# One kernel, three edits: VectorE adds the second bias itself, three gate products in a row, two weights turned a turn later

## The reference, cut to what matters

```python
x = x + _L0_conv_ref(_gn(x), w_qkv, w_dw, w_proj, temperature)
x = x + _L1_conv_ref(_gn(x), gate_w, gate_b, w1, b1, w2, b2)

def _L1_conv_ref(x, gate_w, gate_b, w1, b1, w2, b2):
    scores = _softmax(x_flat @ gate_w + gate_b, -1)
    top_v, top_i = jax.lax.top_k(scores, 2)
    top_w = jax.nn.softmax(top_v, -1)
    present = (top_i[:, :, None] == jnp.arange(4)[None, None, :]).any(0)
    coef = jnp.einsum('ke,kbhw->ebhw', present, top_w)
    hdn = relu(jnp.einsum('bchw,edc->ebdhw', x, w1) + b1)
    y = jnp.einsum('ebdhw,eod->ebohw', hdn, w2) + b2[:, None, :, None, None]
    return jnp.einsum('ebohw,ebhw->bohw', y, coef)
```

## Time and profile before

| | |
|---|---|
| median of 3 runs | 169.03 us (168.38 to 169.12) |
| the profiled execution | 168.52 us, of which the span of the profile is 166.7 |
| busy in the span | PE 149.2 us (89%), DVE 140.5 (84%), ACT 110.8 (66%), POOL 64.6 (39%) |
| TensorE's granted clock | full in all 40 slices |
| HBM traffic | 23 GB/s over the span |

### The profile page before, as it was taken

How to read it: one execution, slowest core, us unless ns; L and a number is a source line. 1 busy time by engine, 2 the same in 40 slices (tenths; PEclk the granted TensorE clock), 3 DMA queues, 4 the chain that set the end, 5 groups by cost and what they waited for, 6 DMA issues and landing times.

```text
span 166.7 us, 3638 instructions
## 1 busy us (share of the span) xinstructions
PE 149.2 (89%) x1291; PEld 118.4 (71%) x1291; DVE 140.5 (84%) x385; ACT 110.8 (66%) x250; POOL 64.6 (39%) x77
## 2 busy tenths in 40 slices
PE   0499899999989999997999999979998979789973
PEld 0499799999989999996999998846653422223321
DVE  2887997769999899899999889766757979999993
ACT  3485298659496493793895638763949699867830
POOL 7040224505237067175167227205125014854530
PEclk9999999999999999999999999999999999999999
DMA  5682123410504105014013000000000000112113
GB/s 139 173 233 63 22 65 96 137 29 4 153 10 128 32 4 150 11 45 118 0 52 116 0 4 0 0 6 0 0 0 0 0 0 4 47 47 88 56 49 94
DMA packets 8698, 9.06 MB, mean 54 GB/s; under 512 B 3624, under 2 KB 7496, under 8 KB 8680
## 3 DMA queue, kind: packets, MB, share of 16 engines
q1 hardware_dynamic: 8536, 8.59, 18.7%
q10 hardware_dynamic: 144, 0.24, 0.5%
HBM read 2.28 MB, written 1.57 MB: 23 GB/s over the span
## 4 chain that ended last, share of the span: by engine, by line
PE 48%; DVE 22%; ACT 13%; issue 5%; POOL 4%; DMA 3%; SPq 1%; DVEq 0%; ACTq 0%
DVE v_acc L1316 6%; PE qk_ps L858 5%; PE qk_ps L860 5%; DVE h_mixed L1597 4%; ACT h_mixed L612 4%; PE mix_ps L976 3%; ACT hidden L584 3%; DMA x_sb<-in_x 2%; PE mix_ps L1142 2%; PE out_ps L953 2%; DVE stats L1270 2%; POOL x_sb L791 2%; PE qk_ps L847 2%; PE qk_ps L849 2%; PE qk_ps L848 2%
## 5 line engine op out<-in xcount | busy, mean ns | idle before, releaser
L1316 DVE SCALAR_TENSOR_TENSOR v_acc<-v_ps,v_taps,v_acc 96x544 f32<-96x544 f32 x60 | 46.6, 777 | 4.8 <-ACT v_acc L480 3.7
L858 PE MATMUL qk_ps<-w_a,x_a 128*128 128x192 f16 x243 | 46.6, 245 | 0.4 <-DMA x_c<-x_lo 0.4
L860 PE MATMUL qk_ps<-w_b,x_b 128*128 128x192 f16 x243 | 46.5, 245 | 0.0
L858 PEld LDWEIGHTS qk_ps<-w_a,x_a 128*128 128x128 f16 x243 | 24.5, 101 | 0.8 <-issue 0.7
L860 PEld LDWEIGHTS qk_ps<-w_b,x_b 128*128 128x128 f16 x243 | 23.6, 97 | 0.3
L1597 DVE TENSOR_TENSOR h_mixed<-h_mixed,hidden 128x512 f32<-128x512 f32 x24 | 21.4, 941 | 1.2 <-ACT h_mixed L612 1.2
L791 POOL TENSOR_TENSOR x_sb<-x_sb,xn 96x512 f32<-96x512 f32 x8 | 14.3, 1788 | 19.6 <-ACT xn L590 19.6
L863 PE MATMUL qk_ps<-w_c,x_c 96*128 96x192 f16 x81 | 20.1, 248 | 0.0
L753 POOL TENSOR_TENSOR sq_sum<-qk_sq 128x384 f32<-128x384 f32 x7 | 7.0, 999 | 29.6 <-ACT qk_sq L497 24.9
L556 ACT ACTIVATE sc_exp<-sc_qk,neg_max 96x12 f32<-96x12 f32 x16 | 4.7, 296 | 16.9 <-DVE neg_max L1361 16.9
L762 POOL TENSOR_TENSOR rstd<-var_eps,minus_half 96x2 f32<-96x2 f32 (+2 forms) x9 | 8.5, 944 | 19.1 <-DVE var_eps L1296 19.1
(11 more groups left out here) (228 smaller groups left out, 384.6 us busy)
## 6 DMA issues: line engine op xcount, KB each, us to landing
x_b<-x_a SPq DMA_DIRECT2D x7, 324.0 KB, 3.1
x_sb<-in_x SPq DMA_DIRECT2D x8, 192.0 KB, 3.9
out<-xs SPq DMA_DIRECT2D x7, 192.0 KB, 2.1
x_a<-x_lo SPq DMA_DIRECT2D x7, 108.0 KB, 2.4
x_b<-x_lo SPq DMA_DIRECT2D x7, 108.0 KB, 2.3
x_c<-x_lo SPq DMA_DIRECT2D x21, 36.0 KB, 1.9
w_sb<-in_L_conv_w SPq DMA_DIRECT2D x2, 144.0 KB
cst<-in_consts ACTq DMA_DIRECT2D x1, 236.0 KB, 3.6
```

What stands on the lines that cost most here:

```text
L858: eng.matmul(to, window(x_a[p][:, dx, b], half, dy), w_a[:, t, :], start=(t == 0), stop=False, skip_group_check=True)
L860: mm = eng.matmul(to, window(x_b[p][:, dx, b], half, dy), w_b[:, t, :], start=False, stop=False, skip_group_check=True)
L1316: eng.scalar_tensor_tensor(out=v_acc[i % 3][:, :, :], in0=v_window(dy, dx), scalar=v_taps[:, t:t + 1], in1=v_acc[i % 3][:, :, :], op0=ALU. ...
```

## The change

It has three parts. In the tail `b2_part` is gone from ACT, and the addition from POOL. DVE's new `add_bias(i)` reads w0's bank, multiplies by the first column of `bias_col` and adds `x_sb` in one instruction; `add(i)` also adds the second column. PE now waits for `x1_biased`, which DVE sets, before it overwrites w0's bank. In stage 2 `gate(5)`, `gate(6)` and `gate(7)` stand next to each other on PE, with `first(8)` and `first(9)` behind them, and ACT does the three `high_xn2` before `gate_exps(1)` and `relu(8)`. In stage 1 `prep_w1`, the turning of w1 and w2 and all that belongs to it stand one turn later.

```diff
@@ scalar, stage 1
-                if i == 5:
+                if i == 6:
                     copy_w1()
-                if i == 6:
+                if i == 7:
                     copy_w2()
@@ scalar, stage 2
-            relu(8)
+            high_xn2(5)
+            high_xn2(6)
+            high_xn2(7)
             gate_exps(1)
-            high_xn2(5)
-            relu(9)
-            high_xn2(6)
-            relu(10)
-            high_xn2(7)
-            for h in (11, 12, 13, 14):
+            for h in range(8, 15):
                 relu(h)
@@ scalar, tail
-            eng.wait_ge(bias_ready, 1)
-            bias_tile(0)
             top_exps(1)
             coefs(1)
-            bias_tile(1)
             for i in range(2, PAIRS):
                 if i == 3:
                     take_u(1)
                 coefs(i)
-                bias_tile(i)
@@ gpsimd
-            for i in range(PAIRS):
-                eng.wait_ge(b2_ready, i + 1)
-                eng.tensor_tensor(x_sb[:, i, :], x_sb[:, i, :], b2_part[i % 2][:, :], ALU.add).then_inc(x1_biased, 1)
@@ tensor, tail: weight(i)
-                    eng.wait_ge(b2_ready, i - 1)
+                    eng.wait_ge(x1_biased, i - 1)
@@ vector, stage 1
-                if i == 4:
+                if i == 5:
                     prep_w1()
-                if i == 5:
+                if i == 6:
                     low_w1()
@@ vector, tail
+            def add_bias(i):
+
+                eng.wait_ge(w0_done, i + 1)
+                eng.wait_ge(bias_ready, 1)
+                if i == 0:
+                    eng.wait_ge(x1_done, PAIRS)
+                eng.scalar_tensor_tensor(out=x_sb[:, i, :], in0=w0_ps[i % 2][0:C, :], scalar=bias_col[:, 0:1],
+                                         in1=x_sb[:, i, :], op0=ALU.mult, op1=ALU.add).then_inc(x1_biased, 1)
...
-                eng.tensor_tensor(out_sb[i % 2][:, :], x_sb[:, i, :], y_ps[i % 2][0:C, :], ALU.add).then_inc(y_taken, 1)
+                eng.scalar_tensor_tensor(out=out_sb[i % 2][:, :], in0=y_ps[i % 2][0:C, :], scalar=bias_col[:, 1:2],
+                                         in1=x_sb[:, i, :], op0=ALU.add, op1=ALU.add).then_inc(y_taken, 1)
```

More of the change, by code:

```diff
@@ L181, in build @@
         bias_col = sb("bias_col", [C, 2])
-        b2_part = xn2[0:2]
         h_mixed = [sb(f"h_mixed{p}", [128, MT, T]) for p in range(2)]
@@ L315, in build @@
         coef_set = sem("coef_set")
-        b2_ready = sem("b2_ready")
         x1_biased = sem("x1_biased")
@@ L585, in relu @@
                    .then_inc(hid_by_act, 1)
[L587 to L591, removed]
             def gate_exps(c):
@@ L816, in prepare_w1 @@
                 eng.wait_ge(w1_step, 5)
-                eng.wait_ge(mix_ready, 4)
+                eng.wait_ge(mix_ready, 5)
                 for m in range(MT):
@@ L822, in prepare_w2 @@
             def prepare_w2():
-                eng.wait_ge(mix_ready, 5)
+                eng.wait_ge(mix_ready, 6)
                 for m in range(MT):
@@ L936, in mix_heads @@
                     eng.wait_ge(proj_set, 1)
-                if a == 4:
+                if a == 5:
                     eng.wait_ge(w1_lo_set, 1)
-                if a == 5:
+                if a == 6:
                     eng.wait_ge(w2_set, 1)
@@ L1076, in _ @@
             gate(5, 0, 8, 24)
-            first(8)
             gate(6, 0, 8, 24)
-            first(9)
             gate(7, 0, 8, 24)
-            for h in range(10, 12):
+            for h in range(8, 12):
                 first(h)
@@ L1603, in add @@
                 wait(eng, stored[i % 2], 16 * (i // 2))
-                eng.tensor_tensor(out_sb[i % 2][:, :], x_sb[:, i, :], y_ps[i % 2][0:C, :], ALU.add).then_inc(y_taken, 1)
+                eng.scalar_tensor_tensor(out=out_sb[i % 2][:, :], in0=y_ps[i % 2][0:C, :], scalar=bias_col[:, 1:2],
+                                         in1=x_sb[:, i, :], op0=ALU.add, op1=ALU.add).then_inc(y_taken, 1)
             mix(0)
+            add_bias(0)
             mix(1)
+            add_bias(1)
             gate_weights(1)
@@ L1612, in _ @@
             add(1)
+            add_bias(2)
             for i in range(3, PAIRS):
@@ L1615, in _ @@
                 add(i - 1)
+                add_bias(i)
             for b in range(2):
@@ L1621, in _ @@
                 eng.wait_ge(stored[1], 16 * (PAIRS // 2 - 1))
-                eng.tensor_tensor(out_sb[1][:, t], x_sb[:, PAIRS - 1, t], y_last[b][0:C, t], ALU.add).then_inc(y_taken, 1)
+                eng.scalar_tensor_tensor(out=out_sb[1][:, t], in0=y_last[b][0:C, t], scalar=bias_col[:, 1:2],
+                                         in1=x_sb[:, PAIRS - 1, t], op0=ALU.add, op1=ALU.add).then_inc(y_taken, 1)
 def constants():
```

## The result

The changed kernel has a median of 164.61 us (164.06 to 164.92, four runs); the kernel before, on the same chip, 169.0 (168.38 to 169.12). The ratio is 0.9744, with a 95% interval from 0.9704 to 0.9784: faster. The profiled execution took 164.91 us with a span of 163.1. The forecast was 163.4 with a range from 162.2 to 165.8. The kernel before takes 168.3 to 169.2 us in 31 of its 58 executions beside the experiments, with a mean granted clock of 1.00, and 169.4 to 171.6 in the other 27, with 0.99 or less. Where e7, e8, e10 and e11 were timed its median was 170.78, so the ratios of these four are too low, by somewhat under 1%, to be set beside the others.

A forecast was written before the change was run, and what follows sets the result against it. The prediction took DVE, without a gap in the tail and at times locked out by POOL, as the bound. 168.52 - 3.2 - 1.25 - 1.0 = 163.1 us profiled, plus 0.3 for the median: 163.4, range 162.2 to 165.8.

The forecast's parts named there:

- The tail, 3.2 us: Tail: with POOL silent multiplications stay short, a pair costs DVE 3.12 us for 3.47; gain 3.2 us.
- dear instructions: Rival, tail: the two new DVE instructions cost as much as taps; 165.3 us, chance 0.08.
- long multiplications: Rival, tail: multiplications stay long with POOL silent, something else causing it; about 170.8 us, slower, chance 0.04.
- The gates, 1.25 us: Stage 2: the last gate starts 1.3 us earlier and PE need not wait for a relu; gain 1.25 us.
- PE needs that chain's result only at the counting matmuls behind `first(17)`, over 2 us later, so this is covered: Gates: POOL's stretching of DVE's logits chain stays off the path, as PE needs the result over 2 us later.
- by about 0.4 each: Gates: POOL's three `low_xn2` can stretch up to three small DVE instructions by about 0.4 us each.
- pays POOL's bill: Rival, gates: the stretched instructions reach the path, gain 0.5 instead of 1.25 us; 164.2 us, chance 0.1.
- The weights, 1.0 us: Stage 1: moving `prep_w1` a turn later removes PE's 1.10 us stall at `k_diag`; gain 1.0 us.
- The taps of turn 6 start at 82.0, 0.35 earlier than before: Weights, turn 6: with `prep_w1` behind `head_attn(4)`, DVE's taps start at 82.0, 0.35 us earlier.
- close, but no stall: Weights, turn 6: `k_diag` comes at 87.9 to 88.6, PE wants it at 89.05, so PE does not stall.
- I am wrong if PE waits in turn 6: Stage 1: sign against the forecast, PE waiting in turn 6 or 7.
- The sum: Whole kernel: 168.52 less 3.2, 1.25 and 1.0 gives 163.1 us for the profiled execution.

The follow-up runs named there:

- e7: Changed kernel with VectorE making w1's turned copy (`prep_w1`) ahead of the loop over the turns instead of inside turn 5; 163.25 us, ratio 0.96.
- e8: Changed kernel with GpSimd's last three low halves waiting until VectorE has written the gates' input; 164.53 us, ratio 0.9667.
- e10: Changed kernel with w1's copy early, the logits ahead of w1's low half, and GpSimd's last three low halves behind the gates' input; 164.2 us, ratio 0.9656.
- e11: Changed kernel with its third part undone, w1 and w2 turned and split where the kernel before does it; 165.24 us, ratio 0.9724.
- e1: Kernel before with the tail's edits alone; 165.67 us, ratio 0.9788.
- e4: Changed kernel plus an unused GpSimd addition of two 96 x 512 SBUF tiles for each pair of the tail; 170.53 us, ratio 1.0085.
- e5: Changed kernel plus two unused GpSimd memsets of 96 x 512 for each pair of the tail; 165.0 us, ratio 0.9769.
- e6: Changed kernel with VectorE's channel means and logits ahead of `prep_w1` and `low_w1` in the turn; 164.05 us, ratio 0.9706.
- e2: Kernel before with the new order of gates and halves alone; 168.29 us, ratio 0.9947.
- e3: Kernel before with w1 and w2 turned a turn later alone; 169.03 us, ratio 0.9996.

## Why the prediction held, point by point

- **The tail, 3.2 us: right, 3.37.** All its steps are seen: multiplications under 0.69, the new instruction at 0.74 that occupies 0.66, 3.12 for a pair. The gain is 1.33 from `mix(0)` to `mix(2)`, 1.30 from there to `mix(7)` and 0.74 behind it, where the working has 1.25, 1.31 and 0.75 (3.3 in all, put down as 3.2). PE's wait in `last_second` (0.34) and the recurrence of DVE's rows say that DVE sets the pace, as said. e1 gives it alone, e4 takes it back and more with a POOL addition, and e4 beside e5 shows that POOL's reads are what makes multiplications long. The rivals of dear instructions and of long multiplications are out.
- **The gates, 1.25 us: the move right, the cover wrong, 0.93.** The last gate product ended 1.15 nearer to the last `sq_sum` than before. The step that failed is "PE needs that chain's result only at the counting matmuls behind `first(17)`, over 2 us later, so this is covered", and with it "by about 0.4 each". POOL held `g_in` for 1.0 us more, and behind `g_in` stand `g_exp` on ACT and, in ACT's queue, the relu that PE waits 0.2 us for. I had looked at who needs the result of the chain, not at what is queued behind its middle. PE's waits for a relu there fell from 0.89 to 0.17, not to nothing as I had it. Of the 0.32 that are missing 0.10 are the gate itself (1.15 for 1.25), and the rest is close to that 0.17. This is the rival "pays POOL's bill" in part, at 0.2 to 0.3 and not 0.75. That POOL is the cause is read from this chain and fits e8, where longer comparisons made PE's wait 1.09; no run frees the chain of POOL altogether.
- **The weights, 1.0 us: term mis-sized, 0.63.** The 1.10 at `k_diag` is gone in every profile with the turn. The step that failed is "The taps of turn 6 start at 82.0, 0.35 earlier than before". Counted from the first `norm`, they start at 51.51 in the changed kernel and at 51.09 in the kernel before, 0.4 later. `prep_w1` started 0.2 late and lost 0.66 to POOL, and I had left out the last step of the statistics and the logits behind it, 0.35. From this came the wait that I ruled out ("close, but no stall" looked at `k_diag` alone): 0.51 at the norm's sums behind `take_logits(0)`. "I am wrong if PE waits in turn 6" came true for this term. The cause is `prep_w1` in the turn: without it, in e7, there is no such wait and stage 1 is 0.72 shorter. The wait by itself is the smaller part: e6 takes 0.33 off it, leaves `prep_w1` ahead of the taps and gains 0.12.
- **The sum.** It gave 163.1 for the profiled execution, which took 164.91. Of the 1.8, 1.18 are the start, which the sum took as fixed, 0.37 the weights, 0.32 the gates, 0.14 the way from the last addition to the end, less 0.17 of the tail. The largest part of the miss is thus no step of the change. The range held because it was made wide for its rivals' sake, not for this, which it did not name; that is luck in part.

Left open: why TensorE's full pace comes up to 1.5 us later in some executions, and whether the programs differ in how often. Fourteen profiles, of which the same kernel gave 30.98 and 32.54, don't tell.

## What to carry to other kernels

Look at which of VectorE's instructions take two inputs from SBUF while GpSimd reads it, and count each GpSimd instruction beside them as VectorE time: here giving the saturated engine eight more instructions that read PSUM, and GpSimd none, took 3.4 us off. Where work is moved within a turn, look at every product that waits for anything queued behind it, and not only at the one that had the stall; and put such work where its engine waits anyway (`prep_w1`, 0.7 us). For edits worth under 1 us compare stretches between marks inside the profiles, since the start of the program alone moves by 1.5 us from one execution to the next.

## What the runs showed of the hardware that was not expected

- A GpSimd addition of 1.26 us holds even a VectorE instruction of 16 columns (the cast of e4, 1.18 for 0.17), and one of 0.99 us an operation with a scalar on 3 columns (`w_back`, 0.80 for 0.14), as well as those with two tensors. Making it wait only chooses another victim (e8).
- TensorE's pace in the first 14 us: 0.33 or 0.64 us for the same four matmuls, with PE busy throughout and the granted clock shown as 1.00 in both.
- After a wait of PE of about 1.05 us at the tail's start the granted clock fell to 0.50 (1.2 GHz) for some 3 us in e2, e3, e4 and e11, and after 0.65 us in e8. In the other nine profiles it stayed at 1.00 behind a wait of 1.05 or 0.65 us at the same place. In e11's profile the fall cost 0.43 us, because PE has nearly no spare time in the tail.
